# Attention's output product in three fp32r passes, with its rests made by GpSimd and the first maximum taken a step earlier

## The chip, the cores and the metric

One Trainium2 chip, of which the kernel uses one core. The metric is the device time of one execution in microseconds. The kernel before took 1438.55 us, the median of three runs (1437.63 to 1439.17).

## The reference

Two layers on x of 4 batches by 512 tokens by 256 features. Each is an attention and a feed-forward part, with layer norms between (post-norm). What this case touches is the attention of the first layer, with 16 heads of 128:

```
q = (x @ wq).reshape(B, T, H, Dh)            # 16 heads, Dh = 128
c_kv = x @ w_down                            # latent of 128
kv_up = (c_kv @ w_up).reshape(B, T, H, 2 * Dh)
k, v = kv_up[..., :Dh], kv_up[..., Dh:]
q, k = _apply_rope(q, 0), _apply_rope(k, 0)
scores = einsum('bqhd,bkhd->bhqk', q, k) * scale      # causal mask
attn = softmax(scores)
out = einsum('bhqk,bkhd->bqhd', attn, v).reshape(B, T, H * Dh)
return out @ wo
```

After it come a mixture of low-rank experts (8 experts, 688 wide), a linear attention of 32 heads, and a mixture of 64 experts with 6 per token. All inputs and outputs are fp32.

## The kernel before

**The stage.** The value projection and `wo` are folded into one matrix per head, `U` (128 by 256), made before the loop. The attention then works on the latent: for a head and a batch it takes scores, softmax, the product of the probabilities with the latent (`c_tok`), and then that result times `U`. One head in one batch is a step; there are 64 of them. Eight steps (two heads, four batches) are a pair, and eight pairs are a pass. Pair 0 and pair 7 are written out, pairs 1 to 6 run in a hardware loop. Each engine has its own program, in an order written by hand; they meet by semaphores alone.

**fp32r passes.** A matmul of two fp32 tiles runs as two slow passes (the trace has two records for each). In most places the kernel splits both operands in a high part, rounded to the type fp32r, and a low part, the rest (`whole - high`), and runs three fp32r matmuls instead: high by high, high by low, low by high. Before, the output product with `U` is one of the plain fp32 products.

**One step on TensorE** (`step`, lines 1930 to 1980): scores of tiles 0 and 1 of step s; the product of probabilities and latent of step s-1 (`pv_and`, L1903, L1906, L1909) into bank `BO`; scores of tiles 2 and 3 (all scores are L1942); the output product of step s-1 (`project_out`, L1916), four matmuls of 128x256 from `oT` and `U` into banks `BW` and `BW + 1`; the projection of step s+4, by turns 12 matmuls (queries) and 6 (keys) at L1802; ten transposes of the probabilities (L1977).

**The others.** ScalarE copies `oT` out of PSUM once `pv_and` is done (L760), takes the exponentials (L834), and copies the transposed probabilities as high parts `pT` (L760). VectorE takes the negated row maxima (`top`, L1233), multiplies the projection with the rotary tables (`products`, L1162), adds the output product to `acc` (`add`, L1290), and makes the low parts `pT_low` (L1145). In two steps of each pair (n = 3 and 4) it also splits the weights of the next pair (L1149, L1145), and in the last pair it takes layer norm statistics and splits weights of the next part. GpSimd combines the two products of the rotation into `qT` and `kT`: four subtractions or additions of 64x512 a step (L545, L547). A wait at the head of an engine's queue holds everything behind it.

**Into the next part.** `gu_in` and `dn` are loaded once `U` is done, small weights (`la_in` and others) once all rotations are done (`load_small`), and ScalarE's exponentials of step 61 stand behind the copy of `la`.

Of the kernel before, what the change touches and what calls it, by code (L numbers as in the profile page):

```python
# [15 lines left out]
P = 128  # L16
# [39 lines left out]
def program(nc, io, out):  # L56
    ctx = ExitStack()
    with ctx:
# [38 lines left out]
        U = place("U", 89, [P, HEADS, D])  # L97
        qT = place("qT", 105, [P, 2, BATCH, T])
# [10 lines left out]
        wo = place("wo", 173, [P, HEADS, D])  # L109
# [4 lines left out]
        pT_low = place("pT_low", 185, [P, TPB - 1, T], F32R)  # L114
        pT_end = place("pT_end", 207, [P, P])
        oT = place("oT", 172, [P, T])


        gu_in = place("gu_in", 174, [P, KD, 2, F0])
        lb_in = place("lb_in", 137, [NL, 2, F0])  # L120
        dn = place("dn", 191, [M0, FT0, D + NL])
# [129 lines left out]
        dn_hi, dn_lo, dn_first = wd_hi, wd_lo, 7  # L251
        c_ready, chi_ready, clo_ready, ctok_ready = sem("c_ready"), sem("chi_ready"), sem("clo_ready"), sem("ctok_ready")
# [7 lines left out]
        transposed, pt_copied, pv_done, ot_copied = sem("transposed"), sem("pt_copied"), sem("pv_done"), sem("ot_copied")  # L260
        out_ready, acc_added, rinv_ready = sem("out_ready"), sem("acc_added"), sem("rinv_ready")
# [107 lines left out]
        def xa_bank(b):  # L369
            return 4 if b else 6  # L370
# [5 lines left out]
        def _(sp):  # L376
# [17 lines left out]
            sp.wait_ge(u_ready, 8)  # L394
# [127 lines left out]
        def _(pool):  # L522
# [31 lines left out]

            for idx in range(LOOK):
                rotate((qT, kT)[idx % 2], idx // 2, idx, idx % 2, None)

            def pair(g, first, last):
                for n in range(STEPS - LOOK if last else STEPS):
# [24 lines left out]

            pool.wait_ge(roped, 4 * PROJECTIONS)
# [172 lines left out]
        def _(act):  # L758
# [19 lines left out]

            nc.scalar.dma_start(wd_in[:], io["L0_attn_w_down"].rearrange("(k p) n -> p k n", p=P)).then_inc(wd_loaded, 16)
# [20 lines left out]
            for j in range(8):  # L800
                act.wait_ge(u_ready, j + 1)
                copy(U[:, 2 * j:2 * j + 2, :], ps[:, (6, 7, 0, 1, 4, 5, 6, 7)[j], :].rearrange("p (i l) -> p i l", i=2)).then_inc(u_copied, 1)

# [19 lines left out]
            def step(g, n, first, last):  # L823
# [37 lines left out]
                copy(pT_end[:], ps[:, BW + 1, 3 * P:4 * P]).then_inc(pt_copied, 1)  # L861
                if last and n == 6:
                    x1_halves(0)
# [1638 lines left out]
```

## Time and profile before

| what | value |
|---|---|
| median of three runs | 1438.55 us |
| profiled execution | 1435.82 us |
| its span | 1434.1 us |
| TensorE busy | 1370.7 us, 96% |
| VectorE busy | 964.1 us, 67% |
| ScalarE busy | 595.3 us, 42% |
| GpSimd busy | 552.6 us, 39% |
| chain that ended last | PE 75%, DVE 10%, POOL 4%, ACT 4% |

The engines are PE (TensorE), DVE (VectorE), ACT (ScalarE), POOL (GpSimd) and SP (queue of transfers); PEld is TensorE's weight load. Times in the rows are microseconds from the start of the span. A row of the timeline gives the start, the length, the engine, the line and the operation with its output and input, the count, and in brackets how long the engine sat idle before and who released it. The attention loop runs from about 37 to 634 us of the span.

### The profile page before, as it was taken

What the parts mean: (1) busy time and instruction counts of PE and PEld (TensorE: products, weight loads), DVE (VectorE), ACT (ScalarE), POOL (GpSimd) and SP (SyncE); (2) the same over time, 40 slices, a digit from 0 to 9 for tenths busy, and PEclk for the clock granted to TensorE, in tenths of its full rate; (3) what the DMA queues carried; (4) which work ended last, traced back from release to release, by engine and by line L of the source; (5) the groups of instructions that cost most, each with busy time, mean ns of one, the idle gap of its engine ahead of it and who ended that gap; (6) DMA issues with size and microseconds to landing.
All of it is one profiled execution on the core that took longest, in us unless ns stands there. A gap on an engine that the chain in (4) does not pass through costs nothing.

```text
span 1434.1 us, 24167 instructions
## 1 busy us (share of the span) xinstructions
PE 1370.7 (96%) x8036; PEld 1114.2 (78%) x8036; DVE 964.1 (67%) x2469; ACT 595.3 (42%) x1482; POOL 552.6 (39%) x480
## 2 busy tenths in 40 slices
PE   8999999999999999899999999999999999997995
PEld 7777777778777777678878888788888888874664
DVE  5787777777888777866554567557647646886226
ACT  4444444444445444452332243334333334452232
POOL 3655555555555555400124023513523432304122
PEclk9999999999999999999999999999999999999998
DMA  6000000000002000110000020020020001677994
GB/s 187 1 12 1 12 0 11 0 11 0 11 0 66 10 0 0 19 63 8 0 1 0 3 79 8 16 74 9 9 81 7 7 16 41 161 256 241 290 276 135
DMA packets 67951, 76.14 MB, mean 53 GB/s; under 512 B 14189, under 2 KB 55173, under 8 KB 67877
## 3 DMA queue, kind: packets, MB, share of 16 engines
q1 hardware_dynamic: 56533, 58.36, 14.0%
q10 hardware_dynamic: 8560, 12.36, 2.8%
q0 software_dynamic: 2784, 4.46, 1.5%
q8 instruction: 44, 0.72, 0.2%
q14 instruction: 30, 0.25, 0.1%
HBM read 66.22 MB, written 8.95 MB: 52 GB/s over the span
## 4 chain that ended last, share of the span: by engine, by line
PE 75%; DVE 10%; POOL 4%; ACT 4%; issue 3%; DMA 2%; SPq 1%; POOLq 0%; DVEq 0%; ACTq 0%
PE ps L1802 37%; PE ps L1942 9%; PE ps L1916 7%; PE ps L1903 5%; PE ps L1977 4%; PE ps L1909 2%; PE ps L2160 2%; DMA wo<-in_L_attn_wo_dram 1%; PE ps L2309 1%; PE ps L2387 1%; PE ps L2150 1%; PE ps L2073 1%; PE ps L2074 1%; PE ps L2078 1%; DVE pT_low L1145 1%
## 5 line engine op out<-in xcount | busy, mean ns | idle before, releaser
L834 ACT ACTIVATE probs<-ps,nm 128x128 f32<-128x128 f32 (+3 forms) x256 | 134.2, 526 | 170.7 <-DVE nm L1233 170.6
L671 POOL TENSOR_TENSOR qk<-q,ksb 128x512 f32<-128x512 f32 x64 | 83.3, 1302 | 283.0 <-ACT q L944 210.8
L1145 DVE TENSOR_TENSOR pT_low<-ps,pT 128x384 fp32r<-128x384 f32 (+2 forms) x256 | 99.4, 449 | 114.2 <-ACT pT L760 113.0
L1942 PE MATMUL ps<-kT,qT 128*128 128x128 f32 (+3 forms) x512 | 161.3, 438 | 8.2 <-ACT probs L834 8.1
L1162 DVE TENSOR_TENSOR prod<-ps,rope_sb 128x1024 f32<-128x1024 f32 x128 | 150.3, 1214 | 7.6 <-PE ps L1802 7.6
L545 POOL TENSOR_TENSOR qT<-prod 64x512 f32<-64x512 f32 x64 | 81.0, 1266 | 157.9 <-DVE prod L1162 153.1
L760 ACT ACTIVATE pT<-ps 128x384 fp32r<-128x384 f32 (+2 forms) x256 | 84.8, 416 | 121.1 <-PE ps L1977 121.1
L1916 PEld LDWEIGHTS ps<-U,oT 128*128 128x128 f32 x512 | 97.3, 190 | 40.1 <-issue 19.4
L1233 DVE CUSTOM_DVE_ANT_0 ps<-ps,causal 128x128 f32<-128x128 f32 (+3 forms) x256 | 120.3, 508 | 10.2 <-PE ps L1942 9.3
L1916 PE MATMUL ps<-U,oT 128*128 (+1 forms) x512 | 120.9, 379 | 0.0
L545 POOL TENSOR_TENSOR kT<-prod 64x512 f32<-64x512 f32 x64 | 81.4, 1272 | 99.8 <-DVE prod L1162 97.3
L1802 PEld LDWEIGHTS ps<-kvo,qn 128*128 128x128 f32 x768 | 101.4, 193 | 8.1 <-DVE qn L1145 3.4
L1290 DVE SCALAR_TENSOR_TENSOR acc<-ps,rinv,acc 128x256 f32<-128x256 f32 x256 | 105.8, 474 | 0.0
L1802 PE MATMUL ps<-kvo,qn 128*128 128x256 f32 x768 | 103.6, 285 | 2.3 <-DVE qn L1145 2.3
L1802 PE MATMUL ps<-wq,x2T 128*128 128x512 f32 x384 | 98.4, 391 | 4.9 <-POOL wq L603 4.9
L1802 PE MATMUL ps<-xT,wq 128*128 128x512 f32 x384 | 100.1, 408 | 0.5 <-DVE prod L1162 0.5
L1942 PEld LDWEIGHTS ps<-kT,qT 128*128 128x128 f32 x512 | 77.1, 190 | 30.1 <-ACT probs L834 17.1
L1450 DVE SCALAR_TENSOR_TENSOR k<-ps,k 128x512 fp32r<-128x512 f32 x64 | 43.9, 685 | 81.7 <-ACT k L944 81.6
L1802 PE MATMUL ps<-k,x 128*128 128x512 f32 x384 | 91.6, 394 | 0.2
L1903 PEld LDWEIGHTS ps<-pT,c_tok 128*128 128x128 f32 x384 | 66.2, 188 | 29.8 <-ACT pT L760 24.3
L1802 PEld LDWEIGHTS ps<-wq,x2T 128*128 128x128 f32 x384 | 71.7, 188 | 21.3 <-issue 4.1
L1802 PEld LDWEIGHTS ps<-xT,wq 128*128 128x128 f32 x384 | 74.2, 194 | 15.3 <-DVE prod L1162 1.6
(291 smaller groups left out, 2835.3 us busy)
## 6 DMA issues: line engine op xcount, KB each, us to landing
eg<-in_L_ffn_w_gate_dram SPq DMA_DIRECT2D x16, 704.0 KB
eg<-in_L_ffn_w_up_dram SPq DMA_DIRECT2D x16, 704.0 KB
ed<-in_L_ffn_w_down_dram ACTq DMA_DIRECT2D x10, 640.0 KB
ksb<-ks_dram SPq DMA_DIRECT2D x16, 256.0 KB, 3.3
ed<-in_L_ffn_w_down_dram SPq DMA_DIRECT2D x6, 640.0 KB
rows_dram<-rows ACTq DMA_DIRECT2D x4, 640.0 KB, 8.0
acc<-in_L_attn_x_dram SPq DMA_DIRECT2D x4, 512.0 KB
wq_in<-in_L_attn_wq_dram SPq DMA_DIRECT2D x8, 256.0 KB, 2.9
```

The source lines that it names most:

```text
L545: nc.gpsimd.tensor_tensor(dst[0:64, h, b, :], byc[r, 0, :], bys[r, 1, :], ALU.subtract).then_inc(roped, 1)
L671: nc.gpsimd.tensor_tensor(qk[:], q3[:], ksb[b % 2][:], ALU.mult).then_inc(qk_ready, 1)
L760: return nc.scalar.activation(o, i, ACT.Copy)
L834: nc.scalar.activation(probs[hh][:, off:off + (i + 1) * P], ps[:, BS + i % 2, 0:(i + 1) * P], ACT.Exp, bias=nm[:, hh, i:i + 1], scale=-1.0 ...
L1145: return nc.vector.tensor_tensor(o, whole, hi.bitcast(F32), ALU.subtract)
L1162: nc.vector.tensor_tensor(prod[parity][w][:], ps[:, BA:BA + 2, :], rope[:, w:w + 1, :].broadcast_to([P, 2, T]), ALU.mult).then_inc(product ...
L1233: nc.vector.tensor_tensor_reduce(out=row, in0=row, in1=causal[:, T - (i + 1) * P:T], scale=-1.0, scalar=-MASKED, op0=ALU.add, op1=ALU.min, ...
L1290: nc.vector.scalar_tensor_tensor(out=a, in0=ps[:, BW + i // 2, (i % 2) * D:(i % 2 + 1) * D], scalar=rinv[:, hh, i:i + 1], in1=a, op0=ALU.m ...
L1802: last = pe.matmul(o, lhs(a), rhs(c), start=start and j == 0, stop=stop and j == 2)
L1903: pe.matmul(ps[:, BO, k * P:T], c_tok[h][:, b, k, :], pT[:, k, k * P:T], start=k == 0 and h == 0, stop=False)
L1916: last = pe.matmul(ps[:, BW + i // 2, (i % 2) * D:(i % 2 + 1) * D], oT[:, i * P:(i + 1) * P], U[:, bass.ds(2 * g + n % 2, 1), :], start=Tr ...
L1942: pe.matmul(ps[:, bank, 0:(i + 1) * P], qT[:, hh, b, i * P:(i + 1) * P], kT[:, hh, b, 0:(i + 1) * P], start=True, stop=True).then_inc(scor ...
```

## The change

1. `project_out` becomes three fp32r passes: `oT_high` by `U_high` and by `U_low`, then `oT_low` by `U_high`. Its tiles are taken in the order 2, 3, 0, 1. Tiles 2 and 3 go to bank `BW`, tiles 0 and 1 to `BO`, the bank from which `oT` was copied. So the product into tiles 0 and 1 waits for both copies, and the next `pv_and` waits for all adds of the step before. Bank `BW + 1` is free for the transposes at once.
2. ScalarE copies `oT_high` and then `oT`. GpSimd makes `oT_low` in two subtractions of 128x256, tiles 2 and 3 first, ahead of the step's rotation (`o_rest`).
3. `U_high` is made by ScalarE (128x512 a time) and `U_low` by GpSimd, in place of `U` (`u_rest`): the first part before the loop, the other seven in the steps of pair 0. TensorE waits for all of them at the end of pair 0.
4. VectorE takes the first two maxima of step s+1 in step s, one behind each of the last two rests `pT_low`, and so ahead of the weight splits and the layer norm work.
5. `gu_in` lies where `U` was and is loaded after pair 5; `dn`, `wo` and `pT_low` move; `xa_bank(0)` is 5; ScalarE's first sigmoid waits for the last weight split.

```diff
+            def u_rest(j, turned):
+                pool.wait_ge(roped, 4 * turned)
+                pool.wait_ge(uhi_ready, uhi_first + j + 1)
+                nc.gpsimd.tensor_tensor(U_low[:, 2 * j:2 * j + 2, :], U[:, 2 * j:2 * j + 2, :],
+                                        U_high[:, 2 * j:2 * j + 2, :].bitcast(F32), ALU.subtract).then_inc(ulo_ready, 1)
+
+            def o_rest(s, turned):
+                pool.wait_ge(roped, 4 * turned)
+                pool.wait_ge(ot_copied, 2 * s + 2)
+                for t in (slice(T // 2, T), slice(0, T // 2)):
+                    nc.gpsimd.tensor_tensor(oT_low[:, t], oT[:, t], oT_high[:, t].bitcast(F32), ALU.subtract).then_inc(olo_ready, 1)
...
+                    o_rest(g * STEPS + n, g * STEPS + (LOOK + n))
+                    pool.wait_ge(olo_ready, olo_first + 2 * (g * STEPS + (n + 1)))
                     rotate((qT, kT)[n % 2], b, g * STEPS + (LOOK + n), n % 2, before)
+                    if first and n < HEADS // 2 - 1:
+                        u_rest(n + 1, LOOK + n + 1)
...
                     act.wait_ge(pv_done, s)
+                    copy(oT_high[:], ps[:, BO, :]).then_inc(ot_copied, 1)
                     copy(oT[:], ps[:, BO, :]).then_inc(ot_copied, 1)
...
                     rest(pT_low[:, :, q], ps[:, BW + i - 2, 0:3 * P].rearrange("p (k q) -> p k q", q=P), pT[:, :, q]).then_inc(ptlo_ready, 1)
+                    if following:
+                        top(s + 1, 1 - hh, i - 2)
...
-                pe.wait_ge(ot_copied, s + 1)
-                for i in range(TPB):
-                    last = pe.matmul(ps[:, BW + i // 2, (i % 2) * D:(i % 2 + 1) * D], oT[:, i * P:(i + 1) * P],
-                                     U[:, bass.ds(2 * g + n % 2, 1), :], start=True, stop=True)
+                pe.wait_ge(ot_copied, 2 * s + 1)
+                head = bass.ds(2 * g + n % 2, 1)
+                for j in range(2):
+                    if j:
+                        pe.wait_ge(ot_copied, 2 * s + 2)
+                    for i in OUT_TILES[2 * j:2 * j + 2]:
+                        o, t = ps[:, out_bank(i), (i % 2) * D:(i % 2 + 1) * D], oT_high[:, i * P:(i + 1) * P]
+                        pe.matmul(o, t, U_high[:, head, :], start=i % 2 == 0, stop=False, skip_group_check=True)
+                        pe.matmul(o, t, U_low[:, head, :], start=False, stop=False, skip_group_check=True)
+                    pe.wait_ge(olo_ready, olo_first + 2 * s + j + 1)
+                    for i in OUT_TILES[2 * j:2 * j + 2]:
+                        last = pe.matmul(ps[:, out_bank(i), (i % 2) * D:(i % 2 + 1) * D], oT_low[:, i * P:(i + 1) * P],
+                                         U_high[:, head, :], start=False, stop=True, skip_group_check=True)
...
             pair(0, True, False)
+            pe.wait_ge(ulo_ready, ulo_first + HEADS // 2)
```

Three semaphores serve twice: `olo_ready` is `x_turned`, `ulo_ready` is `c_turned`, `uhi_ready` is `u_copied`, and the rows below show them by the older names.

TensorE in a step of pair 0 before, from the second scores to the projection of the keys:

```order
L1942 MATMUL ps<-kT,qT 128x512 [waits probs_ready]
L1916 MATMUL ps<-U,oT 128x256 [waits ot_copied]
L1916 MATMUL ps<-U,oT 128x256 x3
L1802 MATMUL ps<-cT,wk 128x512 [waits wk_lo,products_ready]
```

The same place now:

```order
L1970 MATMUL ps<-U_high,oT_high 128x256 [waits ot_copied]
L1971 MATMUL ps<-U_low,oT_high 128x256
L1970 MATMUL ps<-U_high,oT_high 128x256
L1971 MATMUL ps<-U_low,oT_high 128x256
L1974 MATMUL ps<-U_high,oT_low 128x256 [waits x_turned]
L1974 MATMUL ps<-U_high,oT_low 128x256
L1970 MATMUL ps<-U_high,oT_high 128x256 [waits ot_copied]
L1971 MATMUL ps<-U_low,oT_high 128x256
L1970 MATMUL ps<-U_high,oT_high 128x256
L1971 MATMUL ps<-U_low,oT_high 128x256
L1974 MATMUL ps<-U_high,oT_low 128x256 [waits x_turned]
L1974 MATMUL ps<-U_high,oT_low 128x256
```

Four matmuls have become twelve, and two waits for GpSimd stand between them where none was.

GpSimd at the end of pair 0 now, the last two rotations of the pair with what stands between them:

```order
L557 TENSOR_TENSOR qT<-prod 64x512 [waits scores_ready,products_ready,x_turned]
L559 TENSOR_TENSOR qT<-prod 64x512
L557 TENSOR_TENSOR qT<-prod 64x512
L559 TENSOR_TENSOR qT<-prod 64x512
L570 TENSOR_TENSOR U_low<-U,U_high 128x512 [waits u_copied,roped]
L577 TENSOR_TENSOR oT_low<-oT,oT_high 128x256 [waits ot_copied,roped]
L577 TENSOR_TENSOR oT_low<-oT,oT_high 128x256
```

The last part of `U_low` stands behind a whole rotation, and TensorE's branch into the loop now waits for it:

```order
L2046 UNCONDITIONAL_BRANCH [waits c_turned]
```

VectorE in step n = 3 of a pair before, from the last rests to the products:

```order
L1145 TENSOR_TENSOR pT_low<-ps,pT 128x3x128 [waits pt_copied] x2
L1148 REGISTER_ALU
L1149 SCALAR_TENSOR_TENSOR wq<-wq_in,wq 128x512 [waits wq_hi]
L1230 REGISTER_ALU
L1233 ISA ps,nm<-ps,causal 128x128 [waits scores_ready]
```

The same place now:

```order
L1190 TENSOR_TENSOR pT_low<-ps,pT 128x3x128 [waits pt_copied]
L1272 REGISTER_ALU
L1275 ISA ps,nm<-ps,causal 128x128 [waits scores_ready]
L1275 ISA nm 128x1
L1190 TENSOR_TENSOR pT_low<-ps,pT 128x3x128 [waits pt_copied]
L1272 REGISTER_ALU
L1275 ISA ps,nm<-ps,causal 128x256 [waits scores_ready]
L1275 ISA nm 128x1
L1193 REGISTER_ALU
L1194 SCALAR_TENSOR_TENSOR wq<-wq_in,wq 128x512 [waits wq_hi]
```

The first maximum has passed the last rest and the split; the second has passed the split.

## Rows read from the trace of the kernel before

**Rows 1.** Windows, 49 steps of the loop: each engine's busy time, clock, DMA.

```profile
113.00:563.00 450.00, 448.84 (x2252) 355.40 (x2251) 356.64 (x943) 219.04 (x696) 249.97 (x196) 1.00 0.04 10
```

**Rows 2.** Chain that ended last, three undisturbed output products: start, length, what.

```profile
407.98 1.73 PE ps L1916 x8
...
417.81 1.73 PE ps L1916 x8
...
426.23 1.73 PE ps L1916 x8
```

**Rows 3.** The same chain in pair 6, around the weight splits.

```profile
509.68 1.73 PE ps L1916 x8
518.56 1.73 PE ps L1916 x8
528.58 1.73 PE ps L1916 x8
```

**Rows 4.** Timeline of DVE behind the rests of step n = 3.

```profile
515.21 0.68 DVE L1149 SCALAR_TENSOR_TENSOR wq<-wq_in,wq 128x512 fp32r<-128x512 f32 x1
515.81 0.29 DVE L1233 CUSTOM_DVE_ANT_0 ps<-ps,causal 128x128 f32<-128x128 f32 x1
```

**Rows 5.** Timeline of one step, from the rests to the output product.

```profile
505.32 1.55 DVE L1145 TENSOR_TENSOR pT_low<-ps,pT 128x256 fp32r<-128x256 f32 x4 [2.64 <-ACT pT L760]
...
507.38 2.35 DVE L1162 TENSOR_TENSOR prod<-ps,rope_sb 128x1024 f32<-128x1024 f32 x2
...
507.41 0.77 PE L1909 MATMUL ps<-pT_low,c_tok 128*128 128x512 f32 x3
...
508.21 0.60 ACT L760 ACTIVATE oT<-ps 128x512 f32<-128x512 f32 x1
...
509.52 1.89 PE L1916 MATMUL ps<-U,oT 128*128 x8
...
509.81 1.26 POOL L545 TENSOR_TENSOR qT<-prod 64x512 f32<-64x512 f32 x1 [4.49 <-DVE prod L1162]
```

**Rows 6.** Page, costliest groups: fp32r matmuls of 128x256 in the linear attention.

```profile
L1802 PE MATMUL ps<-kvo,qn 128*128 128x256 f32 x768 | 103.6, 285 | 2.3 <-DVE qn L1145 2.3
```

**Rows 7.** Timeline of PE, twelve of these matmuls in a row.

```profile
946.05 1.60 PE L1802 MATMUL ps<-kvo,qn 128*128 128x256 f32 x12
```

**Rows 8.** Timeline of ACT, two copies of 512 out of PSUM in a row.

```profile
635.38 1.08 ACT L760 ACTIVATE xaT<-ps 72x512 fp32r<-72x512 f32 x2 [4.34 <-PE ps L2009]
```

**Rows 9.** One line's instructions on POOL: ns min/median/max, first and last start.

```profile
L603 POOL TENSOR_TENSOR wq<-wq_in,wq x16: 722/734/1124, 686.7 to 1151.1; 128x256 fp32r<-128x256 f32 x16
```

**Rows 10.** Groups by form on POOL: busy, mean ns, idle before.

```profile
L603 POOL TENSOR_TENSOR wq<-wq_in,wq 128x256 fp32r<-128x256 f32 x16 | 13.5, 843 | 1.3
```

**Rows 11.** Timeline of PE at the end of pair 0.

```profile
104.81 1.89 PE L1916 MATMUL ps<-U,oT 128*128 128x256 f32 x8
...
109.01 0.82 PE L1942 MATMUL ps<-kT,qT 128*128 128x128 f32 x4
```

**Rows 12.** Timeline of POOL at the end of pair 0, one rotation of four.

```profile
105.09 1.26 POOL L545 TENSOR_TENSOR qT<-prod 64x512 f32<-64x512 f32 x1 [4.49 <-DVE prod L1162]
...
109.14 1.28 POOL L547 TENSOR_TENSOR qT<-prod 64x512 f32<-64x512 f32 x1
```

**Rows 13.** Timeline of PE in the last pair.

```profile
583.74 1.77 PE L1942 MATMUL ps<-kT,qT 128*128 128x384 f32 x4 [1.94 <-ACT probs L834]
...
611.49 1.77 PE L1942 MATMUL ps<-kT,qT 128*128 128x384 f32 x4 [2.49 <-ACT probs L834]
```

**Rows 14.** Chain in the last pair, from the last products to the transfer.

```profile
593.06 2.22 DVE prod L1162 x2
...
606.14 3.14 DMA la_in<-in_L_ffn_A_up_dram
```

**Rows 15.** Timeline of PE near the end, behind its longest gap.

```profile
1325.51 1.94 PE L2387 MATMUL ps<-ed,hET 88*32 88x256 f32 x16 [4.03 <-DVE y_rest L1709]
```

**Rows 16.** Windows, the stretch behind that gap (clock 0.50).

```profile
1323.40:1330.10 6.70, 4.59 (x23) 2.74 (x24) 2.56 (x13) 0.00 (x0) 0.00 (x0) 0.50 1.08 270
```

More of the change, by code:

```diff
@@ L97, in program @@
         U = place("U", 89, [P, HEADS, D])
+        U_low = place("U_low", 89, [P, HEADS, D], F32R)
+        U_high = place("U_high", 174, [P, HEADS, D], F32R)
         qT = place("qT", 105, [P, 2, BATCH, T])
@@ L582, in x2_rest @@
                                         ALU.subtract).then_inc(x2lo_ready, 1)
+            for s in range(PROJECTIONS - LOOK, PROJECTIONS):
+                o_rest(s, PROJECTIONS)
             pool.wait_ge(roped, 4 * PROJECTIONS)
@@ L861, in step @@
                 copy(pT_end[:], ps[:, BW + 1, 3 * P:4 * P]).then_inc(pt_copied, 1)
+                if first and n < HEADS // 2 - 1:
+                    u_high(n + 1)
                 if last and n == 6:
@@ L936, in _ @@
             act.wait_ge(pv_done, STEPS * PAIRS)
+            copy(oT_high[:], ps[:, BO, :]).then_inc(ot_copied, 1)
             copy(oT[:], ps[:, BO, :]).then_inc(ot_copied, 1)
@@ L1228, in step @@
                 hh = n % 2
-                def top(i):
-                    dve.wait_ge(scores_ready, 4 * s + i + 1)
-                    dve.sem_inc(scores_seen, 1)
-                    row = ps[:, BS + i % 2, 0:(i + 1) * P]
-                    nc.vector.tensor_tensor_reduce(out=row, in0=row, in1=causal[:, T - (i + 1) * P:T], scale=-1.0, scalar=-MASKED,
-                                                   op0=ALU.add, op1=ALU.min, accum_out=nm[:, hh, i:i + 1]).then_inc(negmax_ready, 1)
-                top(0)
-                top(1)
+                following = not (last and n == STEPS - 1)
                 if n <= STEPS - LOOK or not last:
                     products(s + (LOOK - 1), (n + 1) % 2, False)
-                top(2)
-                top(3)
+                top(s, hh, 2)
+                top(s, hh, 3)
                 if not (first and n == 0):
@@ L1283, in add @@
                 dve.wait_ge(rinv_ready, s + 1)
-                for i in range(TPB):
-                    dve.wait_ge(out_ready, 2 * s + i // 2 + 1)
-                    if i == 0 and (not isinstance(s, int) or s > 0):
+                for j, i in enumerate(OUT_TILES):
+                    dve.wait_ge(out_ready, 2 * s + j // 2 + 1)
+                    if j == 0 and (not isinstance(s, int) or s > 0):
                         dve.wait_ge(acc_added, 4 * s)
                     a = acc[:, b * TPB + i, :]
-                    nc.vector.scalar_tensor_tensor(out=a, in0=ps[:, BW + i // 2, (i % 2) * D:(i % 2 + 1) * D],
+                    nc.vector.scalar_tensor_tensor(out=a, in0=ps[:, out_bank(i), (i % 2) * D:(i % 2 + 1) * D],
                                                    scalar=rinv[:, hh, i:i + 1], in1=a,
@@ L1952, in step @@
                 scores(3)
+                if first and n == 1:
+                    pe.wait_ge(ulo_ready, ulo_first + 1)
                 if not (first and n == 0):
```

49 lines of the change are left out of this document (36 added, 13 removed).

## The prediction, made before the changed kernel was run

> **What bounds the kernel now.** I read the windows of the attention loop first, because every edit but the moved loads lies there. Over 450 us of it TensorE is busy for 448.8, VectorE for 356.6, ScalarE for 219.0 and GpSimd for 250.0, all at the full clock of 2.4 GHz [rows 1]. The reader should see that there is one full engine and three with room, so time in the middle of the loop is time in TensorE's queue. Then the chain of waits: the output products of undisturbed steps start 9.83 and 8.42 us apart, by turns, as the step projects queries or keys [rows 2]. One product of four plain fp32 matmuls takes 1.73 us of each. Third, the same chain around the weight splits: 8.88 and 10.02 us [rows 3], so 0.46 and 0.19 more. The timeline shows why: VectorE runs the split of `wq` for 0.68 us before it takes the first maximum [rows 4], on which the exponential and so the third scores wait. Last, the last pair, where half the steps have no projection: TensorE sits idle for 1.94 and 2.49 us before the third scores of two steps [rows 13].
>
> **The output product, in the undisturbed step.** Twelve fp32r matmuls of 128x256 in a row take 1.60 us with a tail of 0.28 [rows 6, 7], so each takes (1.60 - 0.28) / 11 = 0.12 us of the queue. Twelve are 1.44 us against 1.73, or 0.29 us less, if nothing waits. But the fifth matmul waits for GpSimd's first half, and so I walk the step of 505 to 511 us [rows 5]:
>
> - The product of probabilities and latent ends at 507.41 + 0.77 = 508.18. ScalarE starts its copy at 508.21. Two such copies take 1.08 us where one takes 0.60 [rows 5, 8], so the second starts 0.48 later: `oT_high` is there at 508.81 and `oT` at 509.29.
> - GpSimd is idle there (4.49 us before 509.81 [rows 5]). It starts 0.08 later, as it does behind the products (507.38 + 2.35 = 509.73, start 509.81): 509.37. A subtraction of 128x256 with an fp32r output takes 0.73 us in the middle case of line 603 [rows 9]. The halves end at 510.10 and 510.83.
> - TensorE comes to the product at 509.52 as before. Four matmuls run to 510.00. The fifth is released at about 510.10 + 0.05 to 0.08, and its weights, which could not be loaded ahead, cost about one more slot of 0.12 (an estimate from the pitch). So matmuls 5 and 6 run from 510.29 to 510.53, 7 to 10 to 511.01. The second half was there at 510.9, and 11 and 12 end at 511.25. Before, the product ended at 509.52 + 1.73 = 511.25.
>
> So the whole gain of 0.29 us is taken by the wait for GpSimd: zero a step. The bounds: if a half took what half a rotation takes, 1.26 / 2 = 0.63 [rows 5], the first wait is 0.10 shorter and the step gains 0.10. If it took the mean of line 603, 0.84 [rows 10], the second wait binds as well: halves at 510.21 and 511.05, end at about 511.45, 0.20 lost. If GpSimd never mattered, the gain is 0.29. Some 57 steps have TensorE as bound, so the ends are -5.7, +11.4 and -16.5 us. I take the middle case of line 603, which is the same instruction at the same size, leaned a little to the faster side because the release may be 0.03 quicker: -1.5 us over all.
>
> The Trainium skill (GPSIMD Engine Reference, "3.1 Elementwise — side-by-side cycle accounting") gives about 2.6 cycles per element at 1.2 GHz for a two-input operation. For 256 elements that would be an estimate of 0.55 us, and by it the step would gain about 0.18 us and the kernel 10 us. The row of the same size says 0.73 and decides.
>
> GpSimd itself has room: two halves (1.46) and a rotation (four operations, about 5.3 us, from 105.09 to 110.42 [rows 12]) are 6.9 us of at least 8.4. The rotation starts at 510.9 in place of 509.8, and what reads it comes two steps later. ScalarE's extra 0.60 us stands in a stretch where it waits for VectorE's third maximum. The wait of `pv_and` for all adds and the order of tiles cost nothing: the adds end some 2 us before it.
>
> **The first maximum moved.** Between the last two rests VectorE now does one maximum, about 0.2 us of queue. The rests ended at 505.32 + 1.55 = 506.87, now at about 507.1, and TensorE needs the last at 507.41 [rows 5]. So nothing is lost. The gain is the stalls of rows 3: 0.46 + 0.19 = 0.65 us in each of six pairs, and I take 0.5 for pair 0: 4.4 us. Bounds: 3.5 if the split now delays the products instead, 5 if the small waits of other steps go too. What is late next is the products, by 0.68 us, and TensorE reads their bank 1.3 us after they end, since they end at 509.73 and the projection starts at 511.25.
>
> **The end of pair 0.** TensorE now waits there for all of `U_low`. Its seventh remaining part stands on GpSimd behind the rotation of step 6 of the pair. That rotation started at 105.09 and the output product of that step at 104.81 [rows 11, 12]. Now GpSimd first makes the halves: they start 0.15 before the product (as 509.37 against 509.52) and end 1.31 behind it, so the rotation runs from about 106.2 to 111.5. One more subtraction of 128x512 (1.28 [rows 12]) ends at 112.9. TensorE's next scores started at 109.01 [rows 11]. It stands still for 3.9 us, once. Bounds: 3.0 if the two small gaps are shorter, 4.5 if `U_low`'s subtraction is as slow as twice 0.73. Nothing hides it: all other engines wait for TensorE then. The earlier parts of `U_low` just fit: 1.46 + 5.3 + 1.3 is 8.1 us of 8.42.
>
> A pause of that length can lower the clock. In this trace a gap of 4.03 us near the end was followed by the lower level (1.2 GHz) [rows 15, 16], while the gaps of 1.94 and 2.49 us in the attention left it at 2.4 GHz. The window at the lower level ran 4.6 us past that gap; half of the work in such a time is lost, so at most 2.3 us, at least 0. I take 1.0. The Trainium skill (TensorE: Matmul & The Clock Gate, "HAM oscillation — how this bites in real kernels") warns of just this, a pause in the matmuls after which the engine runs cold; the gap of 4.03 us agrees, the shorter ones do not contradict it.
>
> **The last pair.** The statistics of the layer norm stood between the rests and the first maximum of the next step, and TensorE waited 1.94 us [rows 13]. That gap goes; the projection then waits for the products, which the statistics still delay, and about half of the gap is left as gain: I estimate 1.0 us. So the last products (593.06 [rows 14]), the last rotation, and the transfer of `la_in` that waits for it (606.14) come 1.0 us earlier, and the step behind it starts at 610.5 in place of 611.49. In the four steps without a projection the rests are ready before the product, since the third scores come late there, so each gains up to 0.29 us, and the last transposes no longer wait for the last adds. Against it, the last output product waits for ScalarE and GpSimd, about 0.9 us, and the first sigmoid waits for the last split. Together 2.0 us gained, bounds 0.5 and 3.5.
>
> **The sum.** -1.5 - 4.4 + 3.9 + 1.0 - 2.0 = -3.0 us. The profiled execution took 1435.8 us (span 1434.1), so it would be 1432.8; the median of the runs is 2.7 us above it. I forecast 1438.55 - 3.0 = 1435.5 us.
>
> **The rivals.**
>
> - *GpSimd is quick enough.* The halves take 0.63 us or less, or the release needs no reload of weights. For it: plain operations of 64x512 take 1.26. Against it: line 603's fastest is 0.72 [rows 9]. The step then gains 0.10 to 0.29, on 57 steps 6 to 16 us: about 1427, with 1421 as the far end.
> - *GpSimd binds twice a step (slower than before).* The place is the fifth and the eleventh matmul of each output product. From a half of about 0.80 us on, both waits show, and at 0.84 each step loses 0.20 us: 57 x 0.20 = 11.4 in place of -1.5, so 1448. A release of 0.15 in place of 0.08, at 0.73, gives +0.07 a step and 1441. For it: line 603 has single cases of 1.12. Against it: most of them are 0.72 to 0.74.
> - *The stall at the end of pair 0 is not there*, because GpSimd runs ahead of what I reckon: 1435.5 - 4.9 = 1430.6. Against it: every part of the row is counted from GpSimd's own rows and its queue is in order.
> - *The clock falls in full and the stall is 4.5*: 1435.5 + 1.9 = 1437.4.
> - The change might fail to remove the stall of the splits, if the products become the wait: the sum is then +1.4, or 1440.
>
> **How the numbers follow.** Forecast with its clock variant, 0.50, its own range 1431 to 1440; quick GpSimd 0.20; GpSimd binds 0.20; no stall 0.06; splits keep their price 0.04. The range of 1424 to 1446 leaves out the ends of the second and third case. About 0.2% (2.9 us) is what a measurement can tell from no change. The forecast lies on that edge: 0.24 of its 0.50 is faster, 0.23 within, 0.03 slower. With the quick case and the missing stall, faster has 0.48; within 0.2% has 0.30, with a part of the slower cases; slower 0.22.
>
> **What would show it.** In the changed profile: the output product's matmuls with an idle time of about 0.2 us before L1974, released by GpSimd, and steps still 8.4 and 9.8 us apart (right), or 8.1 and 9.5 (quick) or 8.6 and 10.0 (slow). No idle time before the third scores in steps n = 4 and 5. One gap of 3 to 4.5 us on TensorE near 109 us, ended by `U_low`, with or without a fall of the clock behind it. The output of the last statistics step without the 1.94 us gap. The forecast is wrong in its main term if undisturbed steps differ by more than 0.1 us from before, and wrong in its second if the gap at pair 0 is under 2 us.

## The result and the profile after

| | kernel before | changed kernel |
|---|---|---|
| median of nine runs each, side by side | 1439.17 us | 1442.59 us |
| range of the runs | 1437.63 to 1442.52 | 1441.51 to 1444.01 |
| profiled execution, its span | 1435.82, 1434.1 | 1442.07, 1440.3 |

The ratio is 1.0023, 95% interval 1.0013 to 1.0032: the change costs 3.4 us where the prediction had 3.0 us less. The two profiled executions lie 6.2 us apart, because that of the kernel before (1435.82) was faster than any of the nine runs in the table. The windows of both, cut at the same places of the program (end of pair 0, first products of the router, first low-rank products, a wait in the linear attention, end), show where they part. The columns are the stretch, its length, busy time and instructions of PE, PEld, DVE, ACT and POOL, the clock (1.00 is 2.4 GHz, 0.50 is 1.2 GHz), and the share and GB/s of DMA. First the kernel before:

```profile
0.00:109.01 109.01, 103.75 (x533) 83.48 (x534) 73.69 (x171) 53.33 (x148) 56.38 (x54) 1.00 0.22 66
109.01:625.69 516.68, 508.10 (x2550) 400.48 (x2549) 409.94 (x1092) 256.42 (x805) 272.72 (x215) 1.00 0.04 10
625.69:638.43 12.74, 12.74 (x79) 11.02 (x77) 10.80 (x42) 5.10 (x8) 0.00 (x0) 1.00 0.03 9
638.43:1041.63 403.20, 389.01 (x2358) 332.32 (x2356) 237.48 (x568) 139.61 (x237) 114.57 (x110) 1.00 0.08 24
1041.63:1434.10 392.47, 357.09 (x2524) 286.96 (x2524) 232.25 (x597) 140.84 (x285) 108.92 (x102) 0.96 0.49 137
```

The changed kernel:

```profile
0.00:109.20 109.20, 103.48 (x561) 83.59 (x561) 74.89 (x172) 61.57 (x163) 74.88 (x75) 1.00 0.22 66
109.20:625.61 516.41, 503.14 (x2772) 399.20 (x2773) 411.68 (x1091) 290.92 (x861) 356.48 (x328) 1.00 0.04 10
625.61:640.52 14.91, 13.12 (x82) 10.82 (x81) 12.05 (x44) 5.76 (x10) 1.42 (x2) 1.00 0.03 6
640.52:1043.89 403.37, 388.88 (x2357) 332.32 (x2356) 237.43 (x568) 139.74 (x237) 114.83 (x110) 1.00 0.08 24
1043.89:1440.30 396.41, 358.33 (x2524) 288.21 (x2524) 232.71 (x597) 140.79 (x285) 109.00 (x102) 0.96 0.48 136
```

The differences are +0.19, -0.27, +2.17, +0.17 and +3.94 us. The attention as a whole changes by nothing, gains and losses in it cancel. The 2.17 us stand in one short stretch behind it. The last 3.94 lie in work that the change doesn't touch; the end of this text comes back to them.

Inside the attention, an undisturbed step is as long as before. The four output products shown, one row for the first matmul of each, start 9.86, 8.46 and 9.87 us apart (9.83 and 8.42 in [rows 2]); in the other half of each pair it is 9.79 and 8.39:

```profile
465.09 0.69 PE L1970 MATMUL ps<-U_high,oT_high 128*128 x1
...
474.95 0.69 PE L1970 MATMUL ps<-U_high,oT_high 128*128 x1
...
483.41 0.69 PE L1970 MATMUL ps<-U_high,oT_high 128*128 x1
...
493.28 0.69 PE L1970 MATMUL ps<-U_high,oT_high 128*128 x1
```

One of them in the timeline of all engines, which answers to [rows 5]:

```profile
511.06 0.59 ACT L793 ACTIVATE oT<-ps 128x512 f32<-128x512 f32 x1
...
511.46 0.69 PE L1970 MATMUL ps<-U_high,oT_high 128*128 x1
511.73 1.44 POOL L577 TENSOR_TENSOR oT_low<-oT,oT_high 128x256 fp32r<-128x256 f32 x2 [2.79 <-ACT oT L793]
...
512.22 0.28 PE L1971 MATMUL ps<-U_low,oT_high 128*128 x1
...
512.51 0.30 PEld L1974 LDWEIGHTS ps<-U_high,oT_low 128*128 128x128 f32 x2 [0.22 <-POOL oT_low L577]
512.51 0.50 PE L1974 MATMUL ps<-U_high,oT_low 128*128 x2
...
512.85 0.28 PE L1970 MATMUL ps<-U_high,oT_high 128*128 x1
```

The fourth matmul starts at 512.22, the fifth at 512.51, 0.04 us behind the end of GpSimd's first half (512.47). Without the wait it would have come 0.12 us behind the fourth, as the others do. The seventh starts at 512.85, or 0.63 us behind the fourth, where three places in line are 0.36. So the wait costs 0.27 us here (0.34 in the steps of 8.46 and 9.86), which is what the three passes save. GpSimd's halves take 0.74 us each.

The end of pair 0, which answers to [rows 11, 12]. TensorE stands still for 4.07 us; then the clock is 0.50 for 3.41 us (second fence, windows). The step is 13.87 us long in place of 8.42.

```profile
107.94 1.25 PE L2036 MATMUL ps<-ident,probs 128*128 128x128 f32 x10
113.26 1.65 PE L1999 MATMUL ps<-kT,qT 128*128 128x128 f32 x4 [4.07 <-POOL U_low L570]
```

```profile
109.20:113.26 4.06, 0.00 (x0) 0.01 (x1) 0.94 (x3) 0.76 (x3) 3.53 (x3) 0.94 0.00 0
112.75:116.16 3.41, 2.90 (x8) 2.53 (x9) 1.83 (x6) 0.99 (x4) 0.13 (x1) 0.50 0.01 2
```

The last pair, TensorE, which answers to [rows 13]. The gap of 1.94 us is gone. In its place stand 1.27 us, for GpSimd, which here makes `rstd` of the layer norm (first row) before it gets to the rest, and 1.50; the gap behind the transfer of `la_in` stayed, with 2.75:

```profile
585.05 1.03 POOL L565 TENSOR_TENSOR rstd<-vareps,halfp 128x4 f32<-128x4 f32 x1 [3.10 <-DVE vareps L1267]
...
586.95 0.50 PE L1974 MATMUL ps<-U_high,oT_low 128*128 128x256 f32 x2 [1.27 <-POOL oT_low L577]
...
598.47 0.95 PE L2036 MATMUL ps<-ident,probs 128*128 128x128 f32 x7 [1.50 <-ACT probs L873]
...
612.13 1.34 PE L1999 MATMUL ps<-kT,qT 128*128 128x384 f32 x3 [2.75 <-ACT probs L873]
```

And the short stretch with the 2.17 us, on ScalarE. Before:

```profile
626.65 1.28 ACT L879 ACT_TABLE_LOAD   x1
628.62 0.20 ACT L879 ACTIVATE sig<-ps 128x32 f32<-128x32 f32 x1 [0.68 <-PE ps L1802]
```

Changed:

```profile
630.29 1.28 ACT L923 ACT_TABLE_LOAD   x1 [3.73 <-DVE lb L1190]
631.58 0.20 ACT L923 ACTIVATE sig<-ps 128x32 f32<-128x32 f32 x1
```

Before, ScalarE loads the table of the sigmoid while TensorE still makes the sigmoid's input. Now the new wait stands in front, and the load starts only when VectorE's last split has ended. The routing starts 1.56 us after that split in place of at once.

### The profile page after: what moved, and what is told of

Same layout as the page of the kernel before. It is cut to its first block, busy times and chain, and to the rows that moved or that the text cites. A ratio compares the mean times of both kernels' runs of the same rounds, so it can differ in the third digit from the quotient of the medians.

```text
span 1440.3 us, 25221 instructions
## 1 busy us (share of the span) xinstructions
PE 1366.9 (95%) x8292; PEld 1114.1 (77%) x8292; DVE 968.8 (67%) x2469; ACT 638.8 (44%) x1554; POOL 656.6 (46%) x616
## 4 chain that ended last, share of the span: by engine, by line
PE 38%; DVE 9%; ACT 4%; POOL 4%; issue 2%; DMA 1%; SPq 0%; POOLq 0%; ACTq 0%; DVEq 0%
PE ps L1851 28%; PE ps L2220 2%; PE ps L2369 1%; PE ps L2210 1%; PE ps L2133 1%; PE ps L2447 1%; PE ps L2134 1%; PE ps L2138 1%; POOL wq L636 1%; POOL wo L636 1%; DVE hidT L1444 1%; POOL wo L631 0%; DVE lists L1643 0%; POOL wq L631 0%; POOL qk L704 0%
## 5 line engine op out<-in xcount | busy, mean ns | idle before, releaser
L1190 DVE TENSOR_TENSOR pT_low<-ps,pT 128x384 fp32r<-128x384 f32 (+2 forms) x256 | 104.7, 450 | 105.7 <-ACT pT L793 105.7
L577 POOL TENSOR_TENSOR oT_low<-oT,oT_high 128x256 fp32r<-128x256 f32 x128 | 91.7, 738 | 147.3 <-ACT oT L793 147.2
L1851 PE MATMUL ps<-xT,wq 128*128 128x512 f32 x384 | 94.6, 394 | 0.1
L1970 PE MATMUL ps<-U_high,oT_high 128*128 (+1 forms) x256 | 91.7, 380 | 0.6 <-ACT oT_high L793 0.6
L1952 PE MATMUL ps<-pT,c_tok 128*128 128x512 f32 (+2 forms) x384 | 85.8, 358 | 0.0
```

Of the source, the lines that this page charges most:

```text
L577: nc.gpsimd.tensor_tensor(oT_low[:, t], oT[:, t], oT_high[:, t].bitcast(F32), ALU.subtract).then_inc(olo_ready, 1)
L1190: return nc.vector.tensor_tensor(o, whole, hi.bitcast(F32), ALU.subtract)
L1851: last = pe.matmul(o, lhs(a), rhs(c), start=start and j == 0, stop=stop and j == 2)
L1952: pe.matmul(ps[:, BO, k * P:T], c_tok[h][:, b, k, :], pT[:, k, k * P:T], start=k == 0 and h == 0, stop=False)
L1970: pe.matmul(o, t, U_high[:, head, :], start=i % 2 == 0, stop=False, skip_group_check=True)
```

## The experiments

Each has 4 to 11 runs, side by side with the kernel before. The median of that kernel was 1438.39 us beside "The maximum alone", "The product alone", "Seven rests" and "The sigmoid's tile"; 1438.71 beside "Without the rest", "Both mends" and the first two with the rest on VectorE; and 1439.60 beside "GpSimd later", "GpSimd's rest undivided" and "The splits earlier". The changed kernel did not run in these groups. So "less than the changed kernel" compares distances: each one's from the kernel before beside it. That of the changed kernel is +3.4 us.

### The maximum alone

```diff
+                    if following:
+                        top(s + 1, 1 - hh, i - 2)
```

(in the kernel before, with its two maxima at the start of the step taken out.)

> The kernel before with one part of the change alone: the first two maxima of a step are taken in the step ahead, between VectorE's rests. Theory A (the moved maximum pays where VectorE's splits of the weights stood in its way, and nowhere else): 0.6 us less in each of seven pairs, about 4.2 us less than the kernel before, ratio 0.997. Rival B (the gain per pair that the changed kernel shows comes from the product's shorter waits and not from the maximum): no change, within 0.5 us. Rival C (the maxima now delay VectorE's rests, which TensorE waits for in every step): 0.1 us or more in each of 63 steps, 6 us slower.

Measured: 1432.70 us, ratio 0.9955 (0.9941 to 0.9968), 5.7 us less. In its trace the two steps with the splits are 8.44 and 9.82 us long, as the others (8.42 to 8.45, 9.82 to 9.86), and no wait of TensorE is left in the loop. Theory A held for the steps, B and C are out. The pairs give 0.5 us each, 3.5 in seven; the median gives 2.2 more, and no trace here says from what. So one part of the change is worth more than the whole loses, and the other parts cost about 9 us.

### The product alone

```diff
-                    if following:
-                        top(s + 1, 1 - hh, i - 2)
```

(in the changed kernel, with the two maxima back at the start of the step.)

> The changed kernel with its first two maxima back at the start of the step, so that it differs from the kernel before by the product in three passes alone. Theory A (the product gains nothing in an undisturbed step, costs about 5.4 us at the end of pair 0, with the fall of the clock behind it, and about 2 us at the end of the last pair): 6 to 9 us slower than the kernel before, and the stall in front of the scores at the end of pair 0 is there with 3 to 5 us. Rival B (most of the loss is in how maximum and product work together): within 2 us of the kernel before. Rival C (the product gains in a step, hidden by the moved maximum): faster than before.

Measured: 1455.70 us, ratio 1.0116 (1.0100 to 1.0131), 17.3 us more. A had the sign, not the size. The steps with the splits are 9.92 and 9.98 us in place of 8.88 and 10.01 in each pair of the hardware loop, 6.8 us in six pairs. Another 1.9 are in the same two steps of pair 0. The step at the end of pair 0 is 15.40 us for 8.42, with 6.83 us at half clock, which is 7.0 more and longer than in the changed kernel. The timeline shows what had been missed:

```profile
528.30 1.27 POOL L557 TENSOR_TENSOR qT<-prod 64x512 f32<-64x512 f32 x1
...
529.65 1.28 POOL L559 TENSOR_TENSOR qT<-prod 64x512 f32<-64x512 f32 x1
529.73 1.75 DVE L1194 SCALAR_TENSOR_TENSOR wq<-wq_in,wq 128x512 fp32r<-128x512 f32 x1
...
531.40 0.29 DVE L1275 CUSTOM_DVE_ANT_0 ps<-ps,causal 128x128 f32<-128x128 f32 x1
...
532.38 1.77 PE L1996 MATMUL ps<-kT,qT 128*128 128x384 f32 x4 [1.26 <-ACT probs L873]
```

The split of `wq` takes 1.75 us where it took 0.68 [rows 4]. GpSimd is 1.1 us later in the step with its new work, so its last rotation runs from 529.65 to 530.93, and the split ends 0.55 us behind it, as if it had hardly begun before. The maximum, the exponential and the third scores come 1.07 us later. In the changed kernel the split is stretched too, to 1.21 us, but the first maximum is ahead of it:

```profile
L1194 DVE SCALAR_TENSOR_TENSOR wq<-wq_in,wq x6: 1212/1216/1219, 152.9 to 518.1; 128x512 fp32r<-128x512 f32 x6
```

In the kernel before, the last rotation has ended by then (at 515.12, the split starts at 515.21). The Trainium skill says it as a rule (SBUF — State Buffer, "Who interferes with whom"): a VectorE instruction with two SBUF inputs contends with a GpSimd instruction that reads SBUF, and whichever issues second blocks until the first is done. The split starts 0.08 us into an operation of 1.28 and is 1.07 longer; the trace agrees.

### GpSimd later, nothing else

```diff
+                nc.gpsimd.tensor_tensor(extra[:, 0:3 * DH]..., c, c, ALU.subtract)
```

(in the kernel before, ahead of each rotation.)

> The kernel before with one thing more: ahead of each rotation of the loop GpSimd subtracts 128x384 constants from each other into a spare place, which nobody reads, about 1.1 us. TensorE's, ScalarE's and VectorE's own work is as before. Theory A (a VectorE instruction that reads both its operands from SBUF stands still while a GpSimd instruction runs; so a later GpSimd stretches the split of wq, which in the kernel before lies on TensorE's path): the split of wq takes 1.6 to 1.8 us in place of 0.68, each pair loses about 1 us and the kernel 6 to 7 us, undisturbed steps stay at 8.42 and 9.82: about 1445 us. Rival B (what made the product alone so much slower is ScalarE's second copy, 0.6 us ahead of the third exponential): the split stays 0.68 us and the time is that of the kernel before.

Measured: 1448.56 us, ratio 1.0062 (1.0048 to 1.0076). The extra instruction took 0.83 us, shorter than the 1.1 expected, and the split 1.45 us:

```profile
519.91 1.28 POOL L548 TENSOR_TENSOR qT<-prod 64x512 f32<-64x512 f32 x1
520.30 1.44 DVE L1158 SCALAR_TENSOR_TENSOR wq<-wq_in,wq 128x512 fp32r<-128x512 f32 x1
...
522.64 1.77 PE L1951 MATMUL ps<-kT,qT 128*128 128x384 f32 x4 [0.95 <-ACT probs L843]
```

The split's step is 9.66 us for 8.88, the others 8.42 and 9.82 as before: 0.78 us in each of seven pairs, 5.4 us, where A had 1 us a pair. The spans differ by 9.0; the other 3.6 lie in the last pair, where one step of TensorE is 12.89 us in place of 10.32. Its gap ahead of the third scores is 3.53 us for 2.49, and part of the step is at the lower clock. That GpSimd's later rotations delay the transfer behind them is argued. B is out: ScalarE was unchanged, and the split is long all the same.

### Seven rests in place of eight

```diff
-            pe.wait_ge(ulo_ready, ulo_first + HEADS // 2)
+            pe.wait_ge(ulo_ready, ulo_first + HEADS // 2 - 1)
             with pe.Fori(1, PAIRS - 1) as g:
                 pair(g, False, False)
+            pe.wait_ge(ulo_ready, ulo_first + HEADS // 2)
```

> The changed kernel, in which TensorE waits at the end of pair 0 for seven of the eight rests of U, and for the eighth ahead of the last pair, which alone uses it. Theory A (the 4.06 us gap of TensorE at the end of pair 0 is this wait, and the 3.41 us at half clock come from the gap): no gap there and no fall of the clock, 5.4 us less than the changed kernel, about 1437 us. Rival B (GpSimd is behind all the same, since the eighth rest still stands ahead of its rests of the output: the wait moves into the product of the next step): 1 us less or nothing. Rival C (the gap goes, the clock falls all the same, as a matter of its phase): 3.9 us less.

Measured: 1436.40 us, ratio 0.9984 (0.9975 to 0.9993), 5.4 us less than the changed kernel (2.0 under the kernel before, the changed kernel 3.4 over it). The step at the end of pair 0 is 8.47 us for 13.87, and the clock stays up where it had fallen:

```profile
109.20:113.26 4.06, 4.06 (x24) 3.03 (x22) 3.81 (x10) 3.09 (x11) 3.83 (x4) 1.00 0.02 6
112.75:116.16 3.41, 3.33 (x19) 2.50 (x18) 3.40 (x8) 2.11 (x6) 3.07 (x4) 1.00 0.02 5
```

A held, B and C are out.

### The sigmoid's tile at a free place

```diff
-        sig = place("sig", 99, [P, TPB, E0])
+        sig = place("sig", 101.75, [P, TPB, E0])
...
-                if b == 0:
-                    act.wait_ge(w0_lo, w0_first + 6)
```

> The changed kernel with the tile of the first sigmoid at another place, not over the weights that VectorE still reads there, so that ScalarE does not wait for VectorE's last rest (VectorE itself waits for its own before it writes the next small tile). Theory A (the wait put ScalarE's table load, 1.28 us, behind VectorE's rest, on the path to the first routing): 1.5 to 2.1 us less than the changed kernel. Rival B (VectorE's last rest ends as late anyway and its routing starts then): less than 0.5 us.

Measured: 1439.92 us, ratio 1.0010 (1.0001 to 1.0019), 1.9 us less than the changed kernel. The table load is back ahead of the sigmoid's wait:

```profile
628.67 1.28 ACT L921 ACT_TABLE_LOAD   x1
630.64 0.20 ACT L921 ACTIVATE sig<-ps 128x32 f32<-128x32 f32 x1 [0.68 <-PE ps L1851]
```

From the router's first products (627.72) to the first low-rank products (641.07) it takes 13.35 us in place of 14.91: 1.56 less. Both lie in A's 1.5 to 2.1, and B is out. 0.6 us of the 2.17 are not given back. The timeline of VectorE in the routing shows why; in the changed kernel first, then in the kernel before, the same two operations:

```profile
633.13 0.53 DVE L1375 CAST topf<-topi 128x32 f32<-128x32 uint32 x1
633.69 0.67 DVE L1378 TENSOR_TENSOR one<-iota,topf 128x32 f32<-128x32 f32 x1
```

```profile
631.53 0.18 DVE L1326 CAST topf<-topi 128x32 f32<-128x32 uint32 x1
631.75 0.29 DVE L1329 TENSOR_TENSOR one<-iota,topf 128x32 f32<-128x32 f32 x2
```

GpSimd was idle there before, and now makes its last two rests of the output (1.42 us in the third window above). One of each is 0.35 and 0.48 us longer (a single one of the second takes 0.19 before), and they start with 0.49 and 0.62 us of GpSimd's rests left. The next experiment takes these rests away and leaves the sigmoid's wait: there the two take 0.18 and 0.19 us, and the stretch 14.10 us for 14.91. So GpSimd's rests cost the other part, up to 0.8 us.

### Without the rest of the output

```diff
-                    pe.wait_ge(olo_ready, olo_first + 2 * s + j + 1)
-                        last = pe.matmul(..., oT_low[:, i * P:(i + 1) * P], U_high[:, head, :], ...)
+                        last = pe.matmul(..., oT_high[:, i * P:(i + 1) * P], U_high[:, head, :], ...)
```

(GpSimd's `o_rest` goes too. The low part of the output is left out of the product, so this kernel is for its time alone.)

> The changed kernel without GpSimd's rests of the output: the third pass of the product takes oT_high in the place of oT_low (the same twelve matmuls, another value) and waits for nothing on GpSimd. Theory A (in an undisturbed step the third pass waits 0.29 us for the first half of the rest, and this wait has eaten what the three passes save): 0.29 us less in 56 steps, 16 us less than the changed kernel, with steps of 8.1 and 9.5 us; the gap of 1.27 us in the last pair goes too, and TensorE's gap at the end of pair 0 is shorter, since GpSimd is less behind: 1422 to 1426 us. Rival B (TensorE is not what ends a step; the next wait, for ScalarE's exponentials or its copies of the transposes, takes the place of the one that goes): steps as before, only the stall at pair 0 shrinks, 1438 to 1441 us. Rival C (as A, half of it eaten by the next wait): about 1432 us.

Measured: 1421.90 us, ratio 0.9887 (0.9866 to 0.9908), 20.2 us less than the changed kernel. Undisturbed steps are 8.12 and 9.52 us, 0.30 less than before: the twelve matmuls save what was reckoned, and the wait for GpSimd is all that took it. That is some 17 us in 56 steps; the step at the end of pair 0 is 0.9 us shorter, and the gap of 1.27 us in the last pair is gone. A held.

### GpSimd's rest undivided

```diff
-                for t in (slice(T // 2, T), slice(0, T // 2)):
-                    nc.gpsimd.tensor_tensor(oT_low[:, t], oT[:, t], ...).then_inc(olo_ready, 1)
+                nc.gpsimd.tensor_tensor(oT_low[:], oT[:], ...).then_inc(olo_ready, 2)
```

> The changed kernel with GpSimd's rest of the output undivided, one subtraction of 128x512 (about 1.3 us) in the place of two of 128x256 (0.74 each). Theory A (the third pass starts when GpSimd's piece ends, and nothing hides it): tiles 2 and 3 wait 0.5 to 0.6 us longer, tiles 0 and 1 a little less; some 0.5 us more in each of 56 steps that TensorE bounds, 25 to 35 us slower than the changed kernel. Rival B (GpSimd's wait is hidden by another wait of TensorE in the step): under 5 us slower.

Measured: 1476.76 us, ratio 1.0260 (1.0243 to 1.0278), 34 us more than the changed kernel. Steps are 8.99 to 9.02 and 10.39 to 10.43 us. A held. One rest of 512 takes 1.28 us, 0.54 more than a half, and the steps are 0.56 to 0.60 longer; TensorE (second row) waits for it 46 times in 46 steps of the stretch from 113 to 563 us:

```profile
L576 POOL TENSOR_TENSOR oT_low<-oT,oT_high x46: 1275/1276/1280, 122.0 to 559.5; 128x512 fp32r<-128x512 f32 x46
...
  PE ps L1973: 29.0, 46
```

With the run before it, this shows the wait from both sides: taken away, the step is 0.3 us shorter, and what GpSimd's piece grows by, the step grows by.

### Both mends

> The changed kernel with both mends, TensorE's wait for seven of the eight rests at the end of pair 0 and the tile of the first sigmoid at a free place. Theory A (the two add up): 3.5 to 5.4 us for the first and 1.6 us for the second, 1435 us, which is still above the 1432.7 us of the kernel before with the moved maximum alone, since the product itself brings nothing. Rival B (the product gains in itself, and the two mends are all that hid it): 1432 us or less.

The edits are the two shown above. Measured: 1433.69 us, ratio 0.9966 (0.9955 to 0.9977): 8.4 us less than the changed kernel, where the single runs gave 5.4 and 1.9. They add up, within the intervals. It is level with the maximum alone (1432.70, intervals overlap), so the product in three passes with GpSimd's rests is worth nothing even when nothing else is wrong with it.

### The rest on VectorE

```diff
+            def o_rest(s):
+                dve.wait_ge(ot_copied, s + 1)
+                rest(oT_low[:], ps[:, BO, :], oT_high[:]).then_inc(olo_ready, 1)
...
+                    if w == 0 and s is not None:
+                        o_rest(s)
```

(between the two products of the rotation; GpSimd's `o_rest` and ScalarE's second copy go, but for the last step.)

> The changed kernel with the rest of the output on VectorE, undivided, straight from the value bank between its two rotation products, and without ScalarE's second copy of the output (the last step keeps GpSimd). Theory A (the rest is there before TensorE has done its four matmuls, VectorE's maxima come 0.7 us later but the transposes wait for nothing more): the wait in front of the third pass goes, up to 16 us less in the steps; 1422 to 1430 us with the stall at pair 0 still there, though shorter. Rival B (the later third and fourth maximum delay the exponentials, and the transposes wait for ScalarE): 0.3 to 0.7 us more in each step, 1455 us or more. Rival C (both cancel): 1438 to 1443 us.

Measured: 1430.52 us, ratio 0.9944 (0.9930 to 0.9959), 0.5 us above A's range. Undisturbed steps are 8.12 and 9.52 us. Against it, the stall at pair 0 is still there, and not shorter as A had it but longer: 15.19 us for that step, with 6.83 us at half clock in place of 3.41. The steps with the splits cost again: 8.32 and 10.00.

### The rest on VectorE with both mends

> Both mends and the rest of the output on VectorE together. Theory A (the three passes of the product are worth their time once nothing waits for GpSimd): 16 us less than the kernel with both mends, 1417 to 1425 us, the fastest of all. Rival B (VectorE's place in the step is too full): slower than the kernel with both mends, 1440 us or more.

Measured: 1420.83 us, ratio 0.9880 (0.9863 to 0.9897), 12.9 us less than with the mends alone (A had 16). The product's timeline: the fifth matmul (L1977) comes 0.12 us behind the fourth, with no wait.

```profile
476.55 0.60 ACT L790 ACTIVATE oT_high<-ps 128x512 fp32r<-128x512 f32 x1
477.18 0.69 DVE L1184 TENSOR_TENSOR oT_low<-ps,oT_high 128x512 fp32r<-128x512 f32 x1 [0.29 <-ACT oT_high L790]
...
477.45 0.69 PE L1972 MATMUL ps<-U_high,oT_high 128*128 x1
477.79 1.22 DVE L1205 TENSOR_TENSOR prod<-ps,rope_sb 128x1024 f32<-128x1024 f32 x1
...
478.33 0.40 PE L1977 MATMUL ps<-U_high,oT_low 128*128 x2
```

VectorE reads the value bank itself, so it needs no copy of it, and its one rest of 512 elements is there at 477.87, where GpSimd's first half of 256 ended 1.0 us behind the first matmul. A is short by 3 us. The steps with the splits cost 0.2 and 0.5 us more than the undisturbed ones, 4.9 in seven pairs, which is more than that.

### The splits earlier

```diff
+                if n == 3 and not last:
+                    split_wq(g + 1)
```

(VectorE, now straight behind the reciprocal; ScalarE's halves a step earlier; `wk` likewise in step 4.)

> The kernel with both mends and the rest on VectorE, with the weights of the next pair split earlier: ScalarE's halves at the end of steps 2 and 3, VectorE's behind the reciprocal of steps 3 and 4, where it waits for ScalarE's copies. Theory A (the 0.2 and 0.5 us that steps 3 and 4 still cost are VectorE's splits ahead of the products, and they fit into VectorE's idle time): steps of 8.12 and 9.52 us throughout, 0.7 us less per pair, 4 to 5 us less than that kernel, about 1416 us. Rival B (GpSimd rotates at just that time and holds VectorE's split up by up to 1.3 us, so that the rests of the probabilities come late for TensorE): slower than that kernel by 1 us or more per pair.

Measured: 1418.51 us, ratio 0.9852 (0.9830 to 0.9874). The intervals of this and the last overlap; the steps are 8.36 and 9.52 for 8.32 and 10.00, so 0.44 us of 0.7 a pair are gained, 3 of A's 4 to 5 us. The split starts in a place where it takes 0.66 us, so B did not come. Here it is GpSimd that waits: its rotation starts 0.10 us behind the split (142.31 behind 142.21) and takes 1.70 us in place of 1.28. The same rule of the two engines holds the other way round. This is the fastest of all, 21.1 us under the kernel before.

## Why the prediction was wrong

- *The undisturbed step.* The walk said zero and the steps say zero: 73.03 us for eight steps of an inner pair against 73.64 before, a difference no larger than the 0.65 of the splits. The forecast then leaned 1.5 us to the faster side for a release that may be quicker by 0.03 us. Half of the steps are 0.03 us shorter than before (8.39, 9.79) and half 0.04 longer (8.46, 9.86), so that 1.5 was not there.
- *The first maximum.* Forecast -4.4, of it 0.65 for each of six pairs and 0.5 for pair 0. The six pairs gained 0.61 each, and pair 0, by its steps, 8.46 and 9.91 for 8.79 and 9.92, gained 0.34: -4.0. Right, 0.4 too large. But the reason it held in this kernel is more than the forecast knew: without the moved maximum the splits would have cost about 1.0 us more a pair. The forecast took VectorE's split as 0.68 us whatever GpSimd does.
- *The end of pair 0.* Forecast a stall of 3.9, measured 4.07 idle; forecast 1.0 for the clock. The step is 5.45 longer in all, so the clock took about 1.4. Right in place and kind, 0.5 us too small.
- *The last pair.* This is the step that failed. Forecast: "Against it, the last output product waits for ScalarE and GpSimd, about 0.9 us, and the first sigmoid waits for the last split. Together 2.0 us gained". Up to the router's first products the changed kernel makes up 1.9 us of the 2.0. That it is so near is in part luck: the step that held the gap of 1.94 us is 2.16 shorter (9.86 for 12.02), where 1.0 was forecast, and the new waits of 1.27 and 1.50 us, which were not, took back a part. Then the kernel loses 2.17 in the next 15 us. The wait of the sigmoid for the split was named, and the sum has nothing for it. What was not seen is that ScalarE's table load of 1.28 us stands between the wait and the sigmoid; until now it lay ahead. 1.56 us of the 2.17 are this, by the run with the tile moved; the rest is GpSimd's last two rests, which hold up VectorE's routing. The Trainium skill gives the load at about 1283 ns (ScalarE: Activation LUTs, "What ACT_TABLE_LOAD costs"), and the trace has 1.28 us. The drain of about 1380 ns that the page adds is not seen in these rows, where ScalarE is idle ahead of the load and the sigmoid starts 1.29 us after the load's start.
- *Behind the attention.* Forecast: nothing. The profiled pair differs by 3.94 us in the last 396, with the same work. One piece is seen: a gap of 1.85 us that waits for GpSimd's split of `wq` in the linear attention is followed by the lower clock,

```profile
1040.00:1044.59 4.59, 2.74 (x13) 1.97 (x12) 0.41 (x1) 0.64 (x2) 3.60 (x5) 1.00 0.21 59
1044.59:1048.00 3.41, 3.41 (x10) 2.63 (x9) 0.00 (x0) 0.60 (x1) 0.87 (x1) 0.50 0.84 231
```

while in the kernel before the same gap, 1.67 us long, is not:

```profile
1041.70:1045.10 3.40, 3.40 (x18) 2.92 (x19) 0.00 (x0) 0.95 (x2) 0.93 (x1) 1.00 0.62 210
```

It costs some 1.6 us, and the longer gap 0.2. The fall is also in the trace with seven rests and in none of the other eleven, though five of these have the same gap with 1.82 to 1.84 us. The remaining 2.3 of the 3.94 us are smaller pieces, most of them in the last 200 us. Whether any of this is bound to the change, single traces can't tell, and it stays open. From the first low-rank product to the end, the three traces with the product as before take 795.3 to 796.2 us (795.7 before), and all ten with three passes 797.1 to 799.8 (799.8 for the changed kernel). That speaks for something that came with the product and its moved tiles; but two of the three are of the fastest run of their kernel. By the medians, about 1.3 us are lost behind the attention: 3.4 in all, less the 2.1 up to there.

The sum by the measured sizes is 0 - 4.0 + 5.45 - 1.9 + 2.2, or about +1.7; some 0.4 more are small amounts in the start and in pair 0, which makes the 2.1 of the windows up to the low-rank products (0.19 - 0.27 + 2.17). The medians say +3.4. The forecast of -3.0 was out by 6.4 us: 2.2 behind the last pair, 1.5 of the lean, 0.5 at pair 0, 0.4 in the maximum, 0.1 in the last pair, 0.4 of small amounts, and the 1.3 behind the attention, whose cause is open. Without the first two the sum would have been +0.7, on the slower side.

## What to carry to other kernels

All of this is drawn from one kernel. When a change makes an engine wait, look for what that engine does between the wait and the work: a table load that used to be hidden became part of the path here, at 1.56 us. A rest that is needed within half a microsecond was better made by the engine that can read its source where it lies, here VectorE from PSUM, than by the one with the most free time. And a good edit that ships with a bad one is only seen when each is run alone: the maximum was worth 5.7 us, the product -17, both together -3.4. The two do not add up, since the moved maximum takes the split out of TensorE's way, and with it the time by which GpSimd stretches it.

## What was not expected of the hardware

- VectorE's instruction with two SBUF inputs of 128x512 took 0.68 us with GpSimd at rest and 1.21, 1.45 and 1.74 us when it started with some 0.66, 0.89 and 1.20 us of a GpSimd instruction left. The excess (0.53, 0.77, 1.06) is what was left of GpSimd's instruction, less 0.13. With 0.42 us left, in the run with both mends and the rest on VectorE, it took 0.97, which fits too. When VectorE's instruction was the first by 0.10 us, GpSimd's was the longer one, 1.70 for 1.28 us. Read a VectorE duration beside GpSimd's timeline before it is used as a price.
- One and the same gap of TensorE, in the linear attention, was followed by a lower clock at 1.84 and 1.85 us in two kernels, and not at 1.82 to 1.84 us in five others. Gaps of 1.94, 2.49 and 2.75 us elsewhere were not followed by it. The gap ahead of the third scores in the last pair came with it in seven variants (2.34 to 3.53 us) and not in three others (2.87, 3.05 and 3.70 us). The length of a gap alone does not say whether the clock falls.
- A subtraction of 128x384 on GpSimd whose inputs are one and the same tile took 0.83 us, and one of 128x256 with two inputs 0.74.
